# Moving the operands of TensorE to other places in SBUF: feed-forward tiles at 224 bytes modulo 256, x's parts at 224, the context's at 32

## The reference, cut to what matters

```python
emb = silu(_sin_emb(timestep)) @ W_ada + b_ada
scale, shift = split(emb[:, None, :], 2, axis=-1)
x = _ln(src) * (1.0 + scale) + shift
q, k, v = x @ Wq + bq, x @ Wk + bk, x @ Wv + bv          # 16 heads of 32
scores = einsum('bhqd,bhkd->bhqk', q / sqrt(32), k) + attention_bias
probs = softmax(where(src_mask, -inf, scores))
x = x + (einsum('bhqk,bhkd->bhqd', probs, v) @ Wo + bo)
h = _ln(x) * g2 + beta2
x + _gelu2(h @ W1 + b1) @ W2 + b2                        # _gelu2(x) = x * sigmoid(1.702 x)
```

## Time and profile before

| what | value |
|---|---|
| median of three runs | 2417.2 us (2412.65 to 2418.02) |
| the profiled execution's own time | 2417.7 us |
| its span, first to last instruction | 2415.9 us |
| TensorE busy | 2330.2 us (96%) |
| GpSimd, VectorE, ScalarE busy | 1880.0, 1709.8, 1326.4 us |
| mean granted TensorE clock | 0.99 |
| chain that ended last | TensorE 89%, GpSimd 3%, VectorE 3% |
| stages | setup and attention to 1088 us, first half 1089 to 1779, second half to 2407 |

### The profile page before, as it was taken

How to read it: one execution, slowest core, us unless ns; L and a number is a source line. 1 busy time by engine, 2 the same in 40 slices (tenths; PEclk the granted TensorE clock), 3 DMA queues, 4 the chain that set the end, 5 groups by cost and what they waited for, 6 DMA issues and landing times.

```text
span 2415.9 us, 61264 instructions
## 1 busy us (share of the span) xinstructions
PE 2330.2 (96%) x21034; PEld 2193.0 (91%) x21034; DVE 1709.8 (71%) x2864; ACT 1326.4 (55%) x3663; POOL 1880.0 (78%) x1787
## 2 busy tenths in 40 slices
PE   5999999999999999987999999999989999999998
PEld 3888888888888888877999999999979999999998
DVE  5777777777777777767667676767566776666676
ACT  2666666666666666675555555555544443433443
POOL 3777777777777777779777877777898878888886
PEclk9999999999999999998999999999999999999999
DMA  7344444444444444423343434344365656556564
GB/s 239 112 138 142 142 127 126 135 142 142 129 130 138 142 133 126 122 89 124 137 163 148 154 148 159 142 159 154 138 226 174 204 176 202 189 189 205 188 197 131
DMA packets 289442, 372.13 MB, mean 154 GB/s; under 512 B 29072, under 2 KB 203280, under 8 KB 289232
## 3 DMA queue, kind: packets, MB, share of 16 engines
q1 hardware_dynamic: 289232, 369.44, 46.6%
HBM read 251.68 MB, written 117.70 MB: 153 GB/s over the span
## 4 chain that ended last, share of the span: by engine, by line
PE 89%; POOL 3%; DVE 3%; issue 2%; ACT 1%; DMA 1%; SPq 0%; DVEq 0%; POOLq 0%; ACTq 0%
PE up L1600 13%; PE up L1599 13%; PE up L1601 13%; PE psD L956 5%; PE turn L956 5%; PE turn L958 5%; PE turn L957 5%; PE psD L958 5%; PE psD L957 5%; PE psS L985 4%; PE psS L971 3%; PE psC L995 3%; PE turn L1599 2%; PE turn L1600 2%; PE turn L1601 2%
## 5 line engine op out<-in xcount | busy, mean ns | idle before, releaser
L1599 PE MATMUL up<-T,wc 128*128 128x256 f32 x1792 | 507.5, 283 | 14.5 <-DVE gu L1473 7.7
L1600 PE MATMUL up<-T,wc 128*128 128x256 f32 x1792 | 503.6, 281 | 0.0
L1601 PE MATMUL up<-T,wc 128*128 128x256 f32 x1792 | 502.8, 281 | 0.0
L628 POOL TENSOR_TENSOR s<-s,rinv 128x512 f32<-128x512 f32 x254 | 265.1, 1044 | 229.0 <-DVE rinv L823 228.8
L744 ACT ACTIVATE s<-s,nmx 128x128 f32<-128x128 f32 x1024 | 397.4, 395 | 7.3 <-issue 4.3
L1599 PE MATMUL up<-wc,gs 128*128 128x256 f32 x1280 | 354.5, 277 | 2.4 <-DVE gs L1556 2.4
L1599 PEld LDWEIGHTS up<-T,wc 128*128 128x128 f32 x1792 | 339.0, 189 | 18.3 <-DVE gu L1473 8.9
L1600 PE MATMUL up<-wc,gs 128*128 128x256 f32 x1280 | 354.2, 277 | 0.0
L1601 PE MATMUL up<-wc,gs 128*128 128x256 f32 x1280 | 354.0, 277 | 0.0
L688 POOL TENSOR_TENSOR bias<-bias,mneg 128x512 f32<-128x512 f32 x256 | 335.3, 1332 | 11.2 <-DVE mneg L828 11.2
L1600 PEld LDWEIGHTS up<-T,wc 128*128 128x128 f32 x1792 | 339.2, 189 | 0.0
(11 more groups left out here) (221 smaller groups left out, 7016.5 us busy)
## 6 DMA issues: line engine op xcount, KB each, us to landing
bias<-in_bias SPq DMA_DIRECT2D x128, 512.0 KB, 5.3
gated<-gu SPq DMA_DIRECT2D x128, 512.0 KB, 2.6
adab<-ada_rows SPq DMA_DIRECT2D x64, 512.0 KB, 5.4
gbuf<-gated SPq DMA_DIRECT2D x64, 512.0 KB, 4.0
gu<-gated SPq DMA_DIRECT2D x63, 512.0 KB, 3.8
xin<-in_x SPq DMA_DIRECT2D x32, 512.0 KB, 5.0
resid<-rout SPq DMA_DIRECT2D x64, 256.0 KB, 2.0
r<-resid SPq DMA_DIRECT2D x16, 1024.0 KB, 6.1
```

Of the source, the lines that this page charges most:

```text
L628: eng.tensor_tensor(s[:, b, heads, :], s[:, b, heads, :], rinv[:, b, heads].unsqueeze(2).to_broadcast([P, HG, S]), ALU.mult).then_inc(done, 1)
L1599: pe.matmul(out_ap, sh, mh, start=start, stop=False)
L1600: pe.matmul(out_ap, sh, ml, start=False, stop=False)
L1601: return pe.matmul(out_ap, sl, mh, start=False, stop=stop)
```

## The change

Five filling tiles are added or enlarged and two reserves grow. No instruction changes, nor does the order on any engine. `ahead_xT` puts 32 bytes ahead of xT and of all that lies behind it in attention, `ahead_cT` 128 bytes ahead of cT and rout, `ahead_T1` and `ahead_T0` 192 bytes ahead of T1 and T0 (so also of hTf, b2_bc, p1c and p5c behind T0), and `ahead_wc` grows from 32 to 64 bytes. `end_T1` and `zone` grow by 256 bytes each, which moves all behind them by a multiple of 256.

```diff
         self.mean, self.ve, self.rstd, self.expo = sb("mean", [P, 2]), sb("ve", [P, 2]), sb("rstd", [P, 2]), sb("expo", [P, 2])
+        sb("ahead_xT", [P, 8])
         self.xT = [[sb(f"xT{u}_{n}", [P, self.CH, 2 * P], F32R) for n in ("hi", "lo")] for u in range(2)]
...
         pT = sb("pT", [P, H, P])
+        sb("ahead_cT", [P, 32])
         cT = [sb(f"cT_{n}", [P, G, P], F32R) for n in ("hi", "lo")]
...
-        T1, = at_once(("T1", [P, 2, 7, 2, 2 * P], F32R))
+        _, T1 = at_once(("ahead_T1", [P, 48], F32), ("T1", [P, 2, 7, 2, 2 * P], F32R))
...
-        shared("end_T1", [P, 1024])
+        shared("end_T1", [P, 1088])
...
-        r, T0, hTf, b2_bc, p1c, p5c = at_once(("r", [P, 4, DM], F32), ("T0", [P, 2, 7, 2, 2 * P], F32R), eight("hTf"),
+        r, _, T0, hTf, b2_bc, p1c, p5c = at_once(("r", [P, 4, DM], F32), ("ahead_T0", [P, 48], F32), ("T0", [P, 2, 7, 2, 2 * P], F32R), eight("hTf"),
...
-        shared("zone", [P, 12288])
+        shared("zone", [P, 12352])
...
-        _, wc, gu, s1p = at_once(("ahead_wc", [P, 8], F32), ("wc", [P, 8, 2, 7, 2 * P], F32R), ("gu", [P, 4, 4, 2 * P], F32), ("s1p", [P, 2, 2 * P], F32))
+        _, wc, gu, s1p = at_once(("ahead_wc", [P, 16], F32), ("wc", [P, 8, 2, 7, 2 * P], F32R), ("gu", [P, 4, 4, 2 * P], F32), ("s1p", [P, 2, 2 * P], F32))
```

## The result

The changed kernel took 2449.86 us (median of 4; 2448.44 to 2450.1) against 2415.59 us (median of 4) of the kernel before beside it: a ratio of 1.0131, with a 95% interval of 1.0107 to 1.0156. It is slower by 34 us, where 2395 had been forecast, and lies 9 us above the range.

What follows compares the result with a forecast made beforehand. TensorE was taken as the bound, through the distance between matmul starts. The profiled 2417.7 us less 22.4 from the first feed-forward half, all else 0, gave 2395.3, forecast as 2395 us; range 2375 to 2441 us.

Steps and rivals of the forecast that it cites:

- What bounds the kernel: Whole kernel: TensorE gapless in the long stretches, so time is the number of matmuls times the distance between their starts.
- I take the short pace: First feed-forward half, distance 64 to 224: matmul starts go from 117.8 to 113.3 ns apart, 22.4 us less.
- I take 0: Second feed-forward half, distance 192 to 224: keeps 113.3 ns between starts, no change; bound above 22.4 us more.
- the long pace: Feed-forward matmuls of 256 columns: 117.8 ns between starts, against 113.3 for the short one.
- Rival C: Second half pulled off 113.3 ns between starts, first half stays long: slower, 2440 us; chance 0.18.
- K and Q projections: Attention, distance 192 to 224: 0 taken; bounds 8.4 us less in the loop, 2 us more outside it.
- the case against A: Rival A: attention gains too, 2378 to 2389 us, chance 0.20; against it, the loop stayed long for 43 half steps.
- Transposes and small products: Attention's transposes, score and context products: 0 taken; otherwise each ns on a half step's 16 transposes is 1 us.
- Other engines and DMAs: Operands at 64 go to 96: no loss on GpSimd, DMA transfers hidden by slack, cost 0.
- the worse part of D: Rival: a level no row shows, longer than 117.8 ns between starts, above 2441 us; chance 0.06.
- Rival B: Distance does nothing, the pace is left over from each stretch's start: 2417 us, 2 either way; chance 0.12.
- the prediction's estimate: Both feed-forward halves at the 109.2 ns gap: 68 us less; the prediction noted no 256-column row reaches it.

Runs made afterwards that it cites:

- e3_swap: Only wc moved, by 128 bytes, against the kernel before, exchanging the halves' distances (first 192, second 64): 2437.23 us, ratio 1.0068.
- e2_att: The change's attention edits alone (xT 32 bytes on, cT 160 in all) against the kernel before: 2423.09 us, ratio 1.0036.
- e1_ff: The change's feed-forward edits alone (T 192 bytes on, wc 32) against the kernel before: 2442.51 us, ratio 1.0097.
- e14_best: T at 96, wc and cT at 64, plus one transpose at each odd second-half group's start, against the kernel before: 2430.51 us, ratio 1.004.

## Why the prediction was wrong, step by step

**What bounds the kernel** held. TensorE is busy for all but 2.0 us of the three long stretches, nothing else became late in them, and the time follows the pace: 26.9 us worked out for the second half, 26.1 measured.

**The step that failed** is "I take the short pace" for the first half, because "the nearest row is the second half's, 32 bytes away". It supposed that 32 bytes more change little and that there are two paces only. Neither holds: in the first half, 192 itself is mostly at 117.8 ns (e3_swap), 224 at 118.3, and in the second half 224 at 118.3 although 192, its neighbour, has 113.3. The 22.4 us of gain were 2.4 us of loss. The same step gave "I take 0" for the second half, which was the real cost: 26.1 us. The bound above for it, the long pace (22.4 us), was itself too low by 3.7 us, since the pace of 224 is longer than both paces of before. With the first half's 2.4 and attention's 3.9 us these are the 10 us by which the time lies above C's 2440.

**K and Q projections**: 0, because their own row "is the nearest one and shows both paces". They went to 118.4 ns everywhere, from 114.9 ahead of the loop and 117.7 in it. By these paces they alone lose about 3.7 us (an estimate: 44 matmuls of a half step times 16 times 3.5 ns, and times 43 times 0.65 ns), more than the bound above of 2 us, which knew no pace longer than the long one. V, also taken at 0, went to 394 to 395 ns throughout. Attention together lost 3.9 us (by itself, e2_att: 6 us by the medians). The count behind the bound has a slip besides: 64 half steps less 43 leave 21 outside the loop, not 16. That "the loop held the long one" (the case against A) was so in the trace of before, not in that of e3_swap at the same places.

**Transposes and small products**: 0, and it held (272 ns for s, as before). **Other engines and DMAs**: 0, held in effect; VectorE's busy time in the second half grew under TensorE's cover.

**The rivals.** Rival C had the right mechanism, the second half pulled off a short pace that hangs on the exact place, and the first half not gaining; it gave 2440 us and 0.18. What it lacked is the third pace, which was left to the worse part of D with 0.06, and that is where the time fell. Rival B, that the distance does nothing and the pace is left from the start of each stretch, is wrong for the change (the feed-forward distances alone cost 26 us in e1_ff), but its other part is right at a distance of 192: what e14_best and attention in e3_swap show is exactly that.

**The two rules that the prediction set beside its rows.** By the Trainium skill's page "SBUF — State Buffer", section "Who interferes with whom", TensorE's two ports are independent of each other and it never waits on anyone. By that the distance should do nothing, and the traces disagree: with the same instructions, and the same clock, the second half takes 113.3, 116.7, 118.3 or 120.0 ns by the places of its two operands alone. Whether it is at the ports that the two reads meet, no run shows. The gap of 109.2 ns, which the Trainium skill's page "TensorE: Matmul & The Clock Gate", section "Back-to-back issue gap", gives for 256 columns as that of an isolated matmul and not of a stream with weight loads, was not met as a pace at any of the eleven distances tried; to use it for both halves, as the prediction's estimate did, was to take it for what it isn't.

**What stays open.** Which of the two streams waits, and for what, no run shows. Why 48 is good with wc at 80 and T at 128 and not with both 16 bytes lower, and why T0 and T1 differ at 128 and 160, is open too. That the executions near 2438 us of the kernel before are those with a long second half is worked out, not traced.

## What to carry to other kernels

Where TensorE is gapless and the weights change with every matmul, compute the distance between starts from the timeline (here 113.3 to 120.0 ns for one form, 6%), and list where the moving and the stationary operand start modulo 256. Measure each distance with the real loop before building on it: a neighbour 32 or even 16 bytes away is no guide (192 has 113.3 ns, 176 and 208 have 119), and a value that is good for one loop need not be for the next. If one address shows two paces, look for what interrupts the row of matmuls, compare many executions, and judge a version by its spread as well as its median. A stage's time from one trace of each kernel can differ by which pace the execution took (here 6 us in attention), so compare stages over several traces of the same layout.

## What the runs showed of the hardware that I had not expected

- The pace of one matmul form (128x128 against 256 columns, full clock, no wait) went from 113.33 to 120.0 ns with nothing changed but the distance of its operands. The best, 192, lies in the second half between the 119.3 and 119.2 ns of 176 and 208.
- For 512 columns such edits moved the pace between 228.6 and 233.8 ns; the transposes of 128 columns stayed at 272 ns of duration for distances of 64 and 32.
- A single transpose of 128 columns between matmuls turned the pace from 117.8 to 113.3 ns, and a later one back, at unchanged addresses (one trace, distance 192); the short pace held for the 1344 matmuls between the two, over one more transpose.
- Attention at unchanged places modulo 256 ran its loop's half steps at 15.87 us in one execution and at 15.73 to 15.81 in another (before, e3_swap).
- Moving all three operand tiles by 32 bytes changed nothing that could be told (ratio 0.9997, 0.9966 to 1.0029).
